# Denominators moved behind the first score of key tile 3 in an attention and FFN kernel

## The reference

```
xn  = layernorm(x)
out = x + attention(xn) + ffn(xn)
attention: q = rope(xn Wq), k = rope(xn Wk), v = xn Wv     16 heads of 64, 8 for k and v
           k, v repeated twice along the last axis
           softmax(q k^T * 0.5) v, heads joined, times Wo
ffn:       silu(xn Wg^T) * (xn Wu^T), times Wd^T           hidden size 384, int weights / 127
```

## Time and profile before

| | |
|---|---|
| median of three runs | 1201.25 us |
| the profiled execution: its own time | 1203.45 us |
| its span, first to last instruction | 1201.7 us |
| mean granted TensorE clock | 0.97 |
| TensorE matmul busy | 1138.4 us, 95% |
| VectorE busy | 886.1 us, 74% |
| GpSimd busy | 876.5 us, 73% |
| ScalarE busy | 733.7 us, 61% |
| 512 reductions of a tile of maxima | 1215 ns each |
| 1024 exponentials | 600 ns each |

### The profile page before, as it was taken

The page is one execution under the profiler, slowest core; times in us unless marked ns, Lnnn a source line. Parts: engine busy times, 40 slices in busy tenths (PEclk is TensorE's granted clock), DMA queues, the critical chain, the costliest instruction groups (busy, mean ns, idle before and its releaser), DMA issues.

```text
span 1201.7 us, 20113 instructions
## 1 busy us (share of the span) xinstructions
PE 1138.4 (95%) x6288; PEld 669.7 (56%) x6288; DVE 886.1 (74%) x1009; ACT 733.7 (61%) x1330; POOL 876.5 (73%) x274
## 2 busy tenths in 40 slices
PE   5899999999999999999999999999999999999986
PEld 4787455555655556555555555555555555564532
DVE  6686777777877788776777787766786877776631
ACT  3334566665666666665666666665675666665664
POOL 2222877886887888886887888876888788887776
PEclk9899999999999999998999999998999999998999
DMA  6662707062431617062331617053240717050000
GB/s 223 163 249 97 217 2 218 1 200 54 140 79 34 185 36 217 1 200 53 123 95 20 198 36 217 0 172 81 100 117 5 214 36 216 1 126 2 4 1 17
DMA packets 56293, 124.63 MB, mean 104 GB/s; under 512 B 7968, under 2 KB 19488, under 8 KB 54048
## 3 DMA queue, kind: packets, MB, share of 16 engines
q1 hardware_dynamic: 56224, 123.89, 35.4%
HBM read 53.08 MB, written 10.49 MB: 53 GB/s over the span
## 4 chain that ended last, share of the span: by engine, by line
PE 69%; DVE 8%; SPq 8%; issue 7%; DMA 4%; ACT 2%; POOL 1%; DVEq 0%; POOLq 0%; ACTq 0%
PE bank_o L395 19%; PE bank_s L543 16%; PE scores L380 15%; DVE row_max L854 7%; PE scores L362 6%; SPq L235 6%; PE bank_m L370 3%; PE bank_m L431 2%; PE bank_m L408 2%; PE bank_m L405 2%; ACT prob L800 2%; DMA x_stage<-xT_scratch 2%; PE scores L481 2%; PE bank_s L498 1%; DMA x_all<-x 1%
## 5 line engine op out<-in xcount | busy, mean ns | idle before, releaser
L854 DVE TENSOR_REDUCE row_max<-scores 128x1 f32<-128x1024 f32 x512 | 597.7, 1215 | 237.2 <-PE scores L380 235.9
L800 ACT ACTIVATE prob<-bank_s 128x512 f32<-128x512 f32 x1024 | 595.6, 600 | 288.1 <-PE bank_s L543 246.4
L543 PE MATMUL bank_s<-qk_pack 98*128 98x512 f32 x1024 | 434.1, 440 | 24.9 <-ACT prob L800 15.7
L1049 POOL TENSOR_TENSOR prob_sum<-prob_sum,prob 128x2048 f32<-128x2048 f32 x96 | 439.1, 4574 | 9.3 <-ACT prob L800 0.5
L380 PE MATMUL scores<-qk_pack 96*128 96x512 f32 x1024 | 341.2, 415 | 8.9 <-DVE row_max L854 2.2
L543 PEld LDWEIGHTS bank_s<-qk_pack 98*128 98x128 f32 x1024 | 194.7, 191 | 217.1 <-ACT prob L800 96.7
L395 PE MATMUL bank_o<-prob,v 128*32 128x512 f32 x2048 | 260.3, 628 | 0.0
L1049 POOL TENSOR_TENSOR prob_sum<-prob_sum,prob_pair 128x2048 f32<-128x2048 f32 x32 | 147.0, 4595 | 105.9 <-DVE prob_pair L947 105.9
L380 PEld LDWEIGHTS scores<-qk_pack 96*128 96x128 f32 x1024 | 182.7, 193 | 74.6 <-DVE row_max L854 53.4
L993 POOL TENSOR_TENSOR qk_stage<-rope,qk_stage 128x512 fp32r<-128x512 f32 x64 | 81.8, 1279 | 126.1 <-ACT qk_stage L686 126.1
L1041 POOL TENSOR_TENSOR prob_sum<-prob 128x2048 f32<-128x2048 f32 x32 | 146.7, 4583 | 0.0
(11 more groups left out here) (88 smaller groups left out, 686.1 us busy)
## 6 DMA issues: line engine op xcount, KB each, us to landing
qk_pack<-qk_stage SPq DMA_DIRECT2D x384, 128.0 KB, 3.8
table<-tables SPq DMA_DIRECT2D x16, 2048.0 KB, 10.1
w_stage<-w_scratch SPq DMA_DIRECT2D x14, 640.0 KB, 4.8
v<-v_stage SPq DMA_DIRECT2D x32, 256.0 KB, 3.8
xT_scratch<-xT_hl SPq DMA_DIRECT2D x4, 1024.0 KB, 9.6
x_stage<-xT_scratch SPq DMA_DIRECT2D x4, 1024.0 KB, 5.3
w_scratch<-w_split SPq DMA_DIRECT2D x1, 2560.0 KB, 15.3
x_all<-x SPq DMA_DIRECT2D x4, 512.0 KB, 12.5
```

The costliest lines, as they stand in the source:

```text
L543: mm(bank_s[:, h % 2, :], qk_pack[j][0:SCORE_K, 1, kt // QT, h, (kt % QT) * 128:(kt % QT + 1) * 128], qk_pack[j][0:SCORE_K, 0, t, h, :], s ...
L800: A(prob[:, kt % RING, h, :], bank_s[:, h % 2, :], ACT.Exp).then_inc(prob_ready, 1)
L854: V.tensor_reduce(row_max[:, m:m + 1], scores[:, at:at + 2, :].rearrange("p c k -> p (c k)"), axis=AX.X, op=ALU.max).then_inc(max_read, 1)
L1049: TT(prob_sum[:, t], prob_sum[:, t], part, ALU.add).then_inc(sum_done, 1)
```

## The change

The denominators no longer follow the PV pair of key tile 2 but stand alone behind the first score of key tile 3. The first transposes go from key tile 3 to key tile 4, the second from before the second score of key tile 5 to behind its third. The maxima m6 and m8 to m15 get other places among the scores. ScalarE's copy of the denominators moves from behind its exponential (2,1) to behind (3,0), its spread of the inverses from behind (4,1) to behind (5,1); VectorE's inversion goes from behind reduction 9 to behind reduction 11.

```diff
-INVERT_AFTER = 9
+INVERT_AFTER = 11
@@ TensorE, slot
                     elif kt == 2:
                         maxima()
                         score(kt, 1)
-                        maxima()
                         pv_pair(kt)
+                        score(kt, 2)
+                        maxima()
+                        score(kt, 3)
+                        maxima()
+                    elif kt == 3:
                         if not is_first(u):
                             denominators(u - 1, 1 - t)
+                        score(kt, 1)
+                        maxima()
                         score(kt, 2)
                         maxima()
                         score(kt, 3)
                         maxima()
-                    elif kt == 3:
+                    elif kt == 4:
                         if not is_first(u):
                             transpose_den(u - 1)
                         score(kt, 1)
-                        maxima()
-                        score(kt, 2)
-                        maxima()
-                        score(kt, 3)
-                    elif kt == 4:
-                        maxima()
-                        score(kt, 1)
                         pv_pair(kt)
                         score(kt, 2)
                         maxima()
                         score(kt, 3)
                         maxima()
                     elif kt == 5:
+                        maxima()
+                        score(kt, 1)
+                        maxima()
+                        score(kt, 2)
                         if not is_first(u):
                             transpose_inv(u - 1)
-                        score(kt, 1)
-                        maxima()
-                        score(kt, 2)
-                        maxima()
                         score(kt, 3)
+                        maxima()
@@ ScalarE, slot
                         elif (kt, h) == (2, 1):
                             if staged:
                                 round_hi(1, u + 3, 1 - t, s + 1 + t)
-                            if not first:
-                                read_den(u - 1)
-                        elif (kt, h) == (4, 1) and not first:
+                        elif (kt, h) == (3, 0) and not first:
+                            read_den(u - 1)
+                        elif (kt, h) == (5, 1) and not first:
                             spread_inv(u - 1)
```

More of the change, by code:

```diff
@@ L598, in slot @@
                         score(kt, 1)
-                        maxima()
                         pv_pair(kt)
-                        if not is_first(u):
-                            denominators(u - 1, 1 - t)
                         score(kt, 2)
@@ L608, in slot @@
                         if not is_first(u):
-                            transpose_den(u - 1)
+                            denominators(u - 1, 1 - t)
                         score(kt, 1)
@@ L614, in slot @@
                         score(kt, 3)
+                        maxima()
                     elif kt == 4:
-                        maxima()
+                        if not is_first(u):
+                            transpose_den(u - 1)
                         score(kt, 1)
@@ L623, in slot @@
                     elif kt == 5:
-                        if not is_first(u):
-                            transpose_inv(u - 1)
+                        maxima()
                         score(kt, 1)
@@ L628, in slot @@
                         score(kt, 2)
+                        if not is_first(u):
+                            transpose_inv(u - 1)
+                        score(kt, 3)
                         maxima()
-                        score(kt, 3)
                     elif kt == 6:
```

## The result

The changed kernel takes 1224.03 us, median of 4 runs (1222.46 to 1227.27), the kernel before beside it 1202.42. The ratio is 1.0189, 95% interval 1.0153 to 1.0226: slower by 21.6 us. Forecast was 1228, with 1210 to 1241 as its range.

The account below looks back on a forecast made before the run. TensorE, busy 95%, bounds the kernel, so only its late starts count. +1.17 us per unit over 30 units is 35.1, +1 for end units, -3.5 waits, -6 clock: +26.6 on 1201.25, so 1228, range 1210 to 1241.

Parts of the forecast that it names:

- nothing on TensorE waits for it: ScalarE's wait before the copy of the denominators, 91.9 us in 32 times, was said to hold up no TensorE start.
- The split: Per unit on TensorE: one block of PV pair and denominators becomes two, 0.33 us extra for entering and leaving.
- The waits at m10, m13, m14 and the second transposes: New TensorE waits per unit, with refilling: 0.55+0.10 at m10 and m13, 0.48+0.10 at m14, 0.08+0.11 at the transposes.
- First and last unit: Unit 0 has tiles alone, the last the block alone: together between 0 and 2 us, taken as +1.
- Reloads: At three unit ends behind reloads of x, longer units hide DMA waits, -3.5 us, and half clock behind them, -6.
- the place shown: End of the unit before 548.5: TensorE's 1.62 us wait for the maxima's DMA shrinks to about 0.4, clock holds.
- Only the split is paid: Rival: new TensorE waits just equal the old, 31 x 0.33=+10 us, 1211; chance 0.12.
- The clock falls in the run m11 to m15: Rival: TensorE's clock falls among these tiles, 1.7 us per fall, in every second unit +25, 1253; chance 0.08.
- the Trainium skill's rule on small idles between groups of matmuls: Frequent small TensorE idles make the clock fall repeatedly; judged not to happen at these sizes, waits of 0.55 and 0.48.
- The faster rival: Rival: VectorE catches up, tiles behind the moved block never wait, -0.9 us per unit, 1174; chance 0.04.

Follow-up runs that it names:

- The last unit in the old order: Changed kernel with denominators, transposes and copies of the last unit alone in the order of before: 1222.83 us against 1202.77 for the kernel before, ratio 1.018.

## Why the prediction was right, and where its sizes were off

- The step from ScalarE's large wait to "nothing on TensorE waits for it" held: 27 us less of it brought nothing.
- The split, forecast 0.33 per unit. The rows show its parts: 1.85 for the pair that stands alone, 0.33 into the denominators (743.68 to 744.01), 0.34 for the score behind. As a whole it was not measured by itself; in no run does a unit differ by it alone.
- The waits at m10, m13, m14 and the second transposes came at the forecast times, and m11 and m15 were free. From s(2,1) to the PV pair of key tile 6 the unit shown gets 1.13 longer (16.45 to 17.58), forecast 1.16, and nothing before or behind them, as forecast. The median over the ordinary units is 1.10.
- First and last unit, forecast +1, measured +2.3 with what lies before the first and behind the last: the first +0.81, the last +3.95, and 2.5 back outside them. In the first a DMA wait of 1.98 us before 144.75, behind the first load of x, is gone, and more half clock has come (10.2 us instead of 3.4). The mis-sized term is the last unit: its granted clock is 0.85 where the old order gives 0.94.
- Reloads, forecast -3.5 for the waits and -6 for the clock, -9.5 in all. The three pairs of units at the reloads give, against +1.10 each, -2.2, -3.0 and -5.7: -10.9. The waits went from 1.76, 1.62 and 1.49 to 0.99, none and 0.50, -3.4. The clock behind them, read from the excess of the units behind over 32.65 (1.36, 3.04 and 2.86), gave -7.3.
- At the place shown, the wait was to shrink to 0.4 and vanished. That was chance: the changed kernel's unit in front of it has a stretch of half clock from 525.5 (0.50 over 3.4 us) that the old one lacks, and is 1.7 longer by it. At the third reload it is the other way round: the old unit has half clock from 787.4, the changed one does not. The two cancel in the sum.
- A fourth pair of units, near the end, gives -3.1 and is no reload. In the old profile the clock is at half in it, from 1087.8 for 6.8 us, and in the changed one it is not, behind nearly the same idles. I had not counted it, and nothing shows that it comes from the change: the run "The last unit in the old order", whose order is the changed kernel's up to there, has half clock in this same unit. Of the 5 us between 26.6 and 21.6 this is the largest part; the reloads give 1.4.
- Sum: 33.0+2.3-10.9-3.1=21.3 of the measured 21.6; two more units differ by such stretches, by -1.3 and +1.3. Without the fourth pair, which is luck by all that the runs show, the change would have cost some 24.7 us, nearer to the forecast.
- The rivals. "Only the split is paid" fell with the waits at m13 and m14. "The clock falls in the run m11 to m15", which the Trainium skill's rule on small idles between groups of matmuls (TensorE: Matmul & The Clock Gate, A second HAM failure mode: psum-queue depth-cycling) would allow, did not come about: the waits of the ordinary unit leave the clock at 1.00. The traces agree with the rule in the last unit, where nearly every score has an idle before it, and at the starts of the last units (three in the old kernel, two in the changed one). There the trace of before had it already, which the prediction overlooked when it said that it does not happen at these sizes: behind idles of 0.35, 0.21 and 0.16 before scores the clock is at half from 1121.9 for 3.4 us. The faster rival needed a release earlier than in the rows; m13 starts 0.06 behind the reduction of m11 (752.58+1.22=753.80, tile 753.86), as tiles did before.

## What to carry to other kernels

When one engine is busy 95% of the time, a wait on another engine is worth nothing until a start on the busy one is shown to hang on it. Two buffers cover a run of two tiles; from the third on the slower consumer sets the pace. So where a block may stand depends on how many tiles it leaves in a row: moved without the tiles it cost 0.85 us per unit, moved with them as in the change 1.10, with one tile put forward 0.33, and directly behind m7 with all tiles evened nothing. A cost per unit is not the cost times the units: what the longer unit hides elsewhere has to be read at each place where the fast engine waits for something that doesn't get slower.

## What the runs showed of the hardware that I had not expected

The clock is lost by small idles as well as by one long one, but neither loses it every time. At the reloads a single wait of 1.5 to 1.8 us was followed by half clock for 3.4 to 6.8 us; one of 0.99 us, the largest left there in the changed kernel, was not. At the start of every fourth unit from about 380 us on a score waits 1.7 to 2.0 us for an exponential, and the clock fell there in four of five cases in either kernel. The exception in the old one is the wait of 1.72 before 515.65, and in the changed one that of 1.75 before 802.72.

Small idles did the same. In the last unit idles of only 0.34 to 0.47 us, each followed by one or two scores, came before a stretch with a granted clock of 0.68, while idles of 0.38 and 0.27 with a tile and a score between them left the ordinary unit at 1.00. And idles of 0.35, 0.21 and 0.15 to 0.17 before scores were followed by half clock in the kernel before (at 1121.9) and in the run with the old order in the last unit (at 1107.1), but not in the changed kernel at 1107.6, though TensorE's order in the last two is the same up to there. Windows, in this order, with the one around 515.65 in front:

```profile
513.90:522.00 8.10, 6.38 (x39) 3.81 (x39) 4.38 (x5) 5.57 (x11) 5.43 (x2) 1.00 0.27 81
1121.90:1125.30 3.40, 3.40 (x11) 2.03 (x15) 2.00 (x2) 1.87 (x4) 3.26 (x2) 0.51 0.00 0
1107.10:1110.50 3.40, 3.40 (x16) 1.22 (x18) 2.29 (x2) 1.34 (x3) 3.26 (x2) 0.50 0.02 5
1107.60:1114.40 6.80, 6.75 (x40) 4.39 (x41) 4.43 (x4) 4.41 (x9) 6.66 (x2) 1.00 0.01 2
```

The unit with this start took 33.38 us in the run with the old order in the last unit and 31.81 in the changed kernel. What decides whether the clock falls stays open here.
